# A six-block decoder on one core: order of the keys inside a head, and how the values of the first attention are loaded

## The chip, the cores and the metric

The kernel runs on one core of one Trainium2 chip. The metric is the device time of one launch in microseconds (us). Three runs of the kernel before gave 284.87, 285.77 and 710.45 us; the median is 285.77 us, and the third run is one outlier. A profiled execution was taken apart from them.

## The reference

Eight sequences of 128 tokens with 128 features pass through six blocks; after each block the input is added and the sum is layer-normalised. Only the first block is touched here:

```
xq = einsum('bsh,oh->bso', x, wq)          # 8 x 128 x 1024, the same for xk, xv
xq = xq.reshape(bsz, 16, seqlen, 64)       # no transpose: a plain reshape
scores = softmax(einsum('bhid,bhjd->bhij', xq, xk) * 64 ** -0.5)
out = einsum('bhij,bhjd->bhid', scores, xv).reshape(bsz, seqlen, 1024)
x = layernorm(x + einsum('bso,ho->bsh', out, wo))
```

The reshape has no transpose. So head n of a sequence is made of the eight tokens 8n to 8n+7: its row j is the 64 features of column block c (of 16) of token 8n+t, with j = 16t + c. Softmax and the weighted sum run over all 128 rows of keys, so the rows of the keys may be stored in any order as long as the values have the same one.

The other five blocks are a cross-attention, a gated expert, a causal attention of 16 heads of 8 features, a rotary cross-attention with decay, and a quantised feed-forward.

## The kernel before, in words

Each engine has a program of its own, written out by hand; semaphores join them. Time is counted in ticks t. The first attention works on pairs of sequences p = 0 to 3 (NPAIR), with 32 heads per pair, 4 heads per tick (one quad Q), so 8 ticks per pair (QP) and 32 ticks in all. Projections of pair p+1 stand in the ticks of pair p, by the table PJ: i = 0 to 3 are the four projections of the keys, 4 to 7 those of the queries, 8 to 11 those of the values. Ticks 0 and 1 of a pair hold the four of the keys, 2 and 3 those of the queries, 3, 4 and 7 those of the values. Pair 0 is projected before tick 0.

For a projection of keys or queries TensorE (`project`, L618 to L620) writes 512 columns of one PSUM bank. ScalarE (`empty_projection`, L1056) copies it as f16 into the upper halves, VectorE (`lower_parts`, L1305) subtracts that from the PSUM value and stores the rest as f16: what the f16 could not hold. Both do this in two instructions per projection of 64 partitions x 512 elements, one for each half of the column blocks (a = 0, 1). A pair has 8 such instructions for the keys on each engine, and 8 for the queries; four pairs have 64 on each. Two PSUM banks are used in turn: project(i) waits until VectorE has done projection i-2.

The keys lie in KA (upper parts in partitions 0 to 63, lower parts in 64 to 127), the queries in QS; both are parts of the tile `arena`. The view `by_column` says where an element goes. A column block is c = 8a + g. Inside a head of 128 elements, before, the order is (a, g, t): t runs fastest, so eight tokens are 16 bytes in a row. Every read of KA or QS by TensorE is a whole head, so it does not depend on the order inside it.

SyncE (SP) issues all DMAs, one after the other. For each pair: copies of KA into KB with the halves swapped (L374, L376); two stores of the values from VN to `v_piece` in HBM (L383); then for each half h of the heads the loads into V (L390), eight per half, one for each t, each of 16 column blocks x 16 heads x 64 elements into the partitions t, 8+t, 16+t and so on. The partitions of V are the key rows in the order of KA. TensorE's `weigh` (L665) multiplies the exponentials (PT) with V and waits for a half's loads through `v_load`, at 128 per pair (8 x 16).

Behind the last pair's V loads SP goes on to the second attention: constants `later` into the stacks of its first group (L400, waits for `sk_done` 24), stores of its keys and queries (L404, L407, wait for `kp_hi`, `qp_hi` and so on), and, when the stores have landed, loads into the stacks (L410, L414). TensorE's first scores of that attention (`scores1`, L782) wait for all of them at tick 32. Group means the sequences 0 to 2; mid(g, i) are the steps of blocks 2 and 3 of group g, which stand between the others by the table PLACES.

Of the kernel before, what the change touches and what calls it, by code (L numbers as in the profile page):

```python
# [14 lines left out]
P = 128  # L15
NB = 8
NTOK = NB * P
H = 16
DH0 = 64
G = 8  # L20
# [33 lines left out]
def decoder(nc, x_tok, x_T, ctx_T, wq0, wk0, wv0, wo0, xwq0, xbq0, xwk0, xbk0, xwv0, xbv0,  # L54
# [6 lines left out]
    with ExitStack() as ctx:  # L61
# [123 lines left out]

            return buf[:, n * P:(n + 1) * P]

        def by_column(buf, i):

            v = buf.rearrange("p (n a g t) -> p a g n t", a=2, g=G, t=8)  # L190
            return v[:, :, 2 * (i % 4):2 * (i % 4) + 2, :, :]

        def bank(i):
# [5 lines left out]
        def s(name):  # L199

            if name not in named:
                named[name] = sem(name)
            return named[name]
# [114 lines left out]

        def v_there(p, q):

            return s(f"v_load{p % 2}{q // 4}"), 128 * (p // 2 + 1)

        def projected_at(p, i):

# [14 lines left out]
        def _(sp):  # L339
# [31 lines left out]
            for p in range(NPAIR):  # L371
                b = p % 2
                sp.wait_ge(s("qk_hi"), 8 * p + 4)
                sp.dma_start(KB[b][64:P, :], KA[b][0:64, :]).then_inc(qk_in[b], 16)  # L374
                sp.wait_ge(*((pj_free[1], 6 * (p - 1) + 2) if p else (s("qk_lo"), 4)))
                sp.dma_start(KB[b][0:64, :], KA[b][64:P, :]).then_inc(qk_in[b], 16)  # L376
                if p == 1:
                    load_first()
                if p == 2:
                    load_rest()  # L380
                for h in range(2):
                    sp.wait_ge(*((pj_free[1], 6 * (p - 1) + 5 + h) if p else (s("vn_in"), 2 * h + 2)))
                    sp.dma_start(v_piece[2 * p + h].rearrange("n (t c) d -> (n t) (c d)", t=8), v_half(h))\  # L383
                        .then_inc(s(f"v_out{h}"), 16)
                for h in range(2):
                    sp.wait_ge(s(f"v_out{h}"), 16 * (p + 1))
                    if p >= 2:
                        sp.wait_ge(s("pv_done"), QP * (p - 1))
                    for t in range(8):
                        sp.dma_start(V[t::8, b, h * H:(h + 1) * H, 0:DH0],  # L390
                                     v_piece[2 * p + h].rearrange("n (t c) d -> t c n d", t=8)[t])\
                            .then_inc(s(f"v_load{b}{h}"), 16)

# [636 lines left out]
        def _(act):  # L1032
# [14 lines left out]
            def empty_projection(p, i):  # L1047
                at = projected_at(p, i)
                src = bank(at).rearrange("p (g n t) -> p g n t", g=2, t=8)
                act.wait_ge(s("proj_done"), NPROJ * p + i + 1)  # L1050
                if i < 8:
                    if p >= 2:
                        act.wait_ge(s("sk_done"), QP * (p - 1))
                    dst = by_column((KA, QS)[i // 4][p % 2][0:64, :], i)
                    for a in range(2):
                        m = fn(dst[:, a], src[a * 64:(a + 1) * 64], ACT.Copy)  # L1056
                    m.then_inc(s("qk_hi"), 1)
                else:
                    h = (i - 8) // 2
                    if p and i % 2 == 0:  # L1060
                        act.wait_ge(s(f"v_out{h}"), 16 * p)
                    fn(v_half(h)[:, (i % 2) * 512:(i % 2) * 512 + 512], bank(at), ACT.Copy)\  # L1062
                        .then_inc(s("vn_in") if p == 0 else pj_free[i % 2], 1)
# [208 lines left out]
        def _(dve):  # L1272
# [27 lines left out]
            def lower_parts(p, i):  # L1300
                src = bank(projected_at(p, i)).rearrange("p (g n t) -> p g n t", g=2, t=8)
                dve.wait_ge(s("qk_hi"), 8 * p + i + 1)
                upper, lower = (by_column((KA, QS)[i // 4][p % 2][x, :], i) for x in (slice(0, 64), slice(64, P)))
                for a in range(2):
                    m = tt(lower[:, a], src[a * 64:(a + 1) * 64], upper[:, a], ALU.subtract)  # L1305
                m.then_inc(s("qk_lo") if p == 0 else pj_free[i % 2], 1)
# [428 lines left out]
```

## Time and profile before

| | us |
|---|---|
| three runs | 284.87, 285.77, 710.45 |
| median | 285.77 |
| profiled execution, whole | 287.07 |
| its span, first to last instruction | 285.3 |
| TensorE busy with matmuls | 232.6 (82%) |
| VectorE busy | 200.9 (70%) |
| ScalarE busy | 153.7 (54%) |
| GpSimd busy | 61.2 (21%) |

The profiled execution was 287.07 us, of which 285.3 us is the span. A busy share is a mean over stages with different limits. So the stages are read one by one: in which an engine is never idle, and where the busiest engine stands waiting, and for whom. In this profile PE is TensorE, DVE VectorE, ACT ScalarE, POOL GpSimd, and SPq the queue on which SyncE issues DMAs.

### The profile page before, as it was taken

To read this page: it belongs to the slowest core of one execution; us is meant where nothing else is said; L and a number is where in the kernel's file an instruction comes from. 1 tells how busy PE (TensorE), PEld (TensorE's weight loads), DVE (VectorE), ACT (ScalarE), POOL (GpSimd) and SP (SyncE) were. 2 spreads that over 40 slices of the span, in tenths; PEclk is the share of its full clock that TensorE was granted. 3 is DMA by queue.
4 is the path that set the end of the run, shared out by engine and by line. 5 is a ranking of instruction groups with operands and counts; after the bars stand their busy time and mean duration, and the time that the engine had idled before them with its cause. 6 is when DMAs were issued, how large, how long until landed. Compare 5 with 4: busy or idle time off the path is not lost.

```text
span 285.3 us, 6881 instructions
## 1 busy us (share of the span) xinstructions
PE 232.6 (82%) x2662; PEld 186.8 (65%) x2662; DVE 200.9 (70%) x535; ACT 153.7 (54%) x288; POOL 61.2 (21%) x108
## 2 busy tenths in 40 slices
PE   1869889989899999997994979979998887765442
PEld 1737767879698896986873847757765755453221
DVE  2695996479855989756443547567777878778896
ACT  4983765385737866463544125645643266551372
POOL 4698000000003001030212031443520101011133
PEclk9959999999999999999998689999999999987555
DMA  6265496147763471044979917920040000000002
GB/s 190 105 147 186 100 241 254 62 105 165 208 186 104 102 167 76 3 124 92 247 194 155 231 28 153 187 68 2 15 107 0 3 3 0 2 0 0 0 10 64
DMA packets 28495, 29.15 MB, mean 102 GB/s; under 512 B 19248, under 2 KB 24496, under 8 KB 27184
## 3 DMA queue, kind: packets, MB, share of 16 engines
q1 hardware_dynamic: 28464, 28.72, 39.6%
q8 instruction: 21, 0.34, 0.5%
q14 instruction: 10, 0.08, 0.1%
HBM read 18.49 MB, written 6.03 MB: 86 GB/s over the span
## 4 chain that ended last, share of the span: by engine, by line
PE 47%; DVE 25%; DMA 8%; ACT 6%; issue 6%; SPq 6%; POOL 1%; POOLq 0%; DVEq 0%
DVE arena L1305 7%; DMA k_piece<-VN 4%; PE PS L665 4%; SPq L390 4%; ACT arena L1056 3%; PE PS L799 3%; PE PS L589 3%; PE PS L692 3%; PE PS L782 2%; PE PS L633 2%; DMA arena<-q_piece 2%; PE PS L779 2%; PE PS L780 2%; PE PS L610 2%; DVE arena L1480 2%
## 5 line engine op out<-in xcount | busy, mean ns | idle before, releaser
L1305 DVE TENSOR_TENSOR arena<-PS,arena 64x512 f16<-64x512 f32 x64 | 44.1, 690 | 9.8 <-ACT arena L1056 8.5
L1056 ACT ACTIVATE arena<-PS 64x512 f16<-64x512 f32 x64 | 37.8, 591 | 11.7 <-PE PS L620 10.6
L494 POOL TENSOR_SCALAR shift<-mv 128x3 f32<-128x3 f32 (+2 forms) x12 | 2.9, 241 | 161.4 <-DVE mv L1357 161.4
L1145 ACT ACTIVATE PT<-PS 128x512 f32<-128x512 f32 x32 | 19.0, 594 | 19.9 <-PE PS L783 19.5
L1442 DVE TENSOR_REDUCE rowmax<-PS 128x4 f32<-128x512 f32 x32 | 21.7, 682 | 10.8 <-PE PS L783 10.7
L618 PE MATMUL PS<-xh,w0l 128*128 128x256 f32 x64 | 20.8, 324 | 7.8 <-DVE w0l L1296 5.7
L665 PE MATMUL PS<-V,PT 128*64 128x68 f32 x512 | 22.7, 232 | 3.0 <-issue 1.8
L1310 DVE TENSOR_REDUCE rowmax<-PS 128x4 f32<-128x512 f32 x32 | 21.7, 683 | 2.9 <-PE PS L634 2.5
L1069 ACT ACTIVATE PT<-PS 128x512 f32<-128x512 f32 x32 | 19.0, 595 | 8.7 <-PE PS L649 7.6
L647 PE MATMUL PS<-arena 128*128 128x128 f16 x128 | 23.3, 221 | 0.1
L649 PE MATMUL PS<-MR,En 128*128 128x128 f16 x128 | 23.1, 219 | 0.0
L648 PE MATMUL PS<-arena 128*128 128x128 f16 x128 | 23.1, 219 | 0.0
L665 PEld LDWEIGHTS PS<-V,PT 128*64 128x64 f32 x512 | 18.2, 139 | 7.1 <-issue 3.1
L618 PEld LDWEIGHTS PS<-xh,w0l 128*128 128x128 f32 x64 | 12.8, 200 | 9.1 <-DVE w0l L1296 5.7
L619 PE MATMUL PS<-xl,w0h 128*128 128x256 f32 x64 | 18.6, 290 | 0.0
L620 PE MATMUL PS<-xh,w0h 128*128 128x256 f32 x64 | 18.5, 290 | 0.0
L633 PE MATMUL PS<-arena 128*128 128x128 f16 x128 | 17.9, 221 | 0.5 <-DVE rowmax L1310 0.5
L780 PE MATMUL PS<-MR,En 128*128 128x128 f16 x128 | 18.0, 221 | 0.0
L634 PE MATMUL PS<-arena 128*128 128x128 f16 x128 | 17.6, 219 | 0.0
L1089 ACT ACTIVATE xt<-res,shift,rstd 128x128 f32<-128x128 f32 x32 | 13.5, 484 | 6.3 <-POOL shift L497 6.2
L692 PE MATMUL PS<-wo,OT 128*128 128x128 f32 x128 | 16.0, 278 | 0.5 <-ACT OT L1079 0.4
L1062 ACT ACTIVATE VN<-PS 128x512 f32<-128x512 f32 x16 | 9.4, 597 | 12.7 <-PE PS L612 12.4
(229 smaller groups left out, 631.7 us busy)
## 6 DMA issues: line engine op xcount, KB each, us to landing
arena<-later SPq DMA_DIRECT2D x4, 1152.0 KB, 10.7
arena<-arena SPq DMA_DIRECT2D x8, 512.0 KB, 5.4
v_piece<-VN SPq DMA_DIRECT2D x8, 512.0 KB, 3.0
V<-v_piece SPq DMA_DIRECT2D x64, 64.0 KB, 2.5
V<-later SPq DMA_DIRECT2D x2, 768.0 KB, 10.9
arena<-k_piece SPq DMA_DIRECT2D x4, 192.0 KB, 4.8
arena<-q_piece SPq DMA_DIRECT2D x4, 192.0 KB, 6.0
q_piece<-VN SPq DMA_DIRECT2D x6, 96.0 KB, 5.7
```

Of the source, the lines that this page charges most:

```text
L618: mm(dst, w0l[:, w, g], xh[:, x], start=True, stop=False)
L633: mm(dst, head(QS[p % 2], n), head(KB[p % 2], n), start=True, stop=False)
L647: mm(dst, head(KB[p % 2], n), head(QS[p % 2], n), start=True, stop=False)
L648: mm(dst, head(KA[p % 2], n), head(QS[p % 2], n), start=False, stop=False)
L649: m = mm(dst, En[:, n % H, :], MR[:, b % 2, :], start=False, stop=True)
L665: m = mm(bank(4)[h * 64:h * 64 + 64, first:first + VN_COLS], PT[:, Q % SLOTS_PT, n * P + a * 64:n * P + a * 64 + 64], V[:, p % 2, 4 * q + ...
L692: m = mm(bank(5)[:, 0:P], OT[:, b % 2, g, :], wo[:, g, :], start=(g == 0), stop=(g == G - 1))
L780: mm(part_, En[:, n, :], MR[:, b % 2, :], start=False, stop=False)
L1056: m = fn(dst[:, a], src[a * 64:(a + 1) * 64], ACT.Copy)
L1305: m = tt(lower[:, a], src[a * 64:(a + 1) * 64], upper[:, a], ALU.subtract)
L1310: V_.reduce_max(rowmax[:, 4 * Q:4 * Q + 4], tok(bank(quad_bank(Q))), AX_X)\
L1442: V_.reduce_max(rowmax[:, b * H + 4 * q:b * H + 4 * q + 4], tok(bank(w % 3)), AX_X)\
```

## The change

The keys get another order inside a head: (t, a, g), which is t x 16 + c, the order of the reference. The queries keep theirs. With that, the 128 rows of a head in `v_piece` are in the order of the partitions of V, and a half's values come by one DMA in place of eight. The semaphore then counts 16 per pair in place of 128.

```
-        def by_column(buf, i):
-            v = buf.rearrange("p (n a g t) -> p a g n t", a=2, g=G, t=8)
+        def by_column(buf, i, keys=False):
+            order = "n t a g" if keys else "n a g t"
+            v = buf.rearrange(f"p ({order}) -> p a g n t", a=2, g=G, t=8)
             return v[:, :, 2 * (i % 4):2 * (i % 4) + 2, :, :]
...
-            return s(f"v_load{p % 2}{q // 4}"), 128 * (p // 2 + 1)
+            return s(f"v_load{p % 2}{q // 4}"), 16 * (p // 2 + 1)
...
-                    for t in range(8):
-                        sp.dma_start(V[t::8, b, h * H:(h + 1) * H, 0:DH0],
-                                     v_piece[2 * p + h].rearrange("n (t c) d -> t c n d", t=8)[t])\
-                            .then_inc(s(f"v_load{b}{h}"), 16)
+                    sp.dma_start(V[:, b, h * H:(h + 1) * H, 0:DH0], v_piece[2 * p + h].rearrange("n j d -> j n d"))\
+                        .then_inc(s(f"v_load{b}{h}"), 16)
...
-                    dst = by_column((KA, QS)[i // 4][p % 2][0:64, :], i)
+                    dst = by_column((KA, QS)[i // 4][p % 2][0:64, :], i, i < 4)
...
-                upper, lower = (by_column((KA, QS)[i // 4][p % 2][x, :], i) for x in (slice(0, 64), slice(64, P)))
+                upper, lower = (by_column((KA, QS)[i // 4][p % 2][x, :], i, i < 4) for x in (slice(0, 64), slice(64, P)))
```

In the view of the keys one instruction now steps 16 f16 elements (32 bytes) from each element to the next, where eight neighbours stood together before. The number of elements and of bytes is the same everywhere, and a packet of the V loads stays one row of 64 f32, 256 bytes.

On SP's queue, in the program of the last pair and the start of the second attention's first group, this stood before (V is loaded from v_piece, `later` holds constants of the stacks):

```order
L383 DMA v_piece<-VN 128x1024 x2
L390 DMA V<-v_piece 16x16x64 x16
L400 DMA arena<-later 96x6144 x2
L404 DMA k_piece<-VN 128x384 x2
L407 DMA q_piece<-VN 128x384 x3
```

and this stands there now:

```order
L390 DMA V<-v_piece 128x16x64 x2
L399 DMA arena<-later 96x6144 x2
L403 DMA k_piece<-VN 128x384 x2
L406 DMA q_piece<-VN 128x384 x3
L409 DMA arena<-k_piece 16x6144 x2
```

Fourteen issues are gone ahead of the constants; nothing has changed its place. (Line numbers behind the V loads are one lower in the new file.)

On DVE's queue, at the start (pair 0's lower parts, the first maxima, then pair 1's first lower parts), this stood before:

```order
L1305 TENSOR_TENSOR arena<-PS,arena 64x2x32x8 x16
L1310 TENSOR_REDUCE rowmax<-PS 128x4 x5
L1316 TENSOR_SCALAR MR<-PS 16x128
L1317 SCALAR_TENSOR_TENSOR MR<-PS,MR 16x128
L1305 TENSOR_TENSOR arena<-PS,arena 64x2x32x8 x4
L1310 TENSOR_REDUCE rowmax<-PS 128x4
```

and this stands there now:

```order
L1304 TENSOR_TENSOR arena<-PS,arena 64x2x256 x8
L1304 TENSOR_TENSOR arena<-PS,arena 64x2x32x8 x8
L1309 TENSOR_REDUCE rowmax<-PS 128x4 x5
L1315 TENSOR_SCALAR MR<-PS 16x128
L1316 SCALAR_TENSOR_TENSOR MR<-PS,MR 16x128
L1304 TENSOR_TENSOR arena<-PS,arena 64x2x256 x4
```

The instructions are as many and in the same order; those of the keys have another form: 2 x 256 elements at an even step in place of 2 x 32 runs of 8. ScalarE's queue changes in the same way.

## Rows read from the trace of the kernel before

**Rows 1.** The chain that ended last, shares of the span by line (the page).

```profile
DVE arena L1305 7%; DMA k_piece<-VN 4%; PE PS L665 4%; SPq L390 4%; ACT arena L1056 3%; PE PS L799 3%; PE PS L589 3%; PE PS L692 3%; PE PS L782 2%; PE PS L633 2%; DMA arena<-q_piece 2%; PE PS L779 2%; PE PS L780 2%; PE PS L610 2%; DVE arena L1480 2%
```

**Rows 2.** Busy time of DVE in five stretches: from:to, length, busy, PE clock, DMA.

```profile
9.30:21.20 11.90, 11.04 (x16) 0.76 0.39 90
28.20:43.40 15.20, 14.19 (x24) 1.00 0.70 174
43.40:58.80 15.40, 7.48 (x20) 1.00 0.42 152
58.80:75.20 16.40, 14.94 (x27) 1.00 0.67 161
92.80:110.30 17.50, 16.13 (x31) 1.00 0.47 110
```

**Rows 3.** Timeline of SP, 123 to 136 us: start, length, line, what.

```profile
123.54 11.20 SPq L390 DMA_DIRECT2D V<-v_piece  x16
134.79 1.06 SPq L400 DMA_DIRECT2D arena<-later  x2
```

**Rows 4.** The chain in order of time, 136 to 164 us.

```profile
136.36 11.61 DMA k_piece<-VN
150.63 5.91 DMA arena<-q_piece
158.47 0.85 PE PS L709 x3
```

**Rows 5.** Timeline of PE and ACT: in brackets the idle time before, and its releaser.

```profile
131.71 0.69 PE L665 MATMUL PS<-V,PT 128*64 128x68 f32 x16 [1.78 <-issue]
155.36 1.26 ACT L1089 ACTIVATE xt<-res,shift,rstd 128x128 f32<-128x128 f32 x3 [1.47 <-POOL shift L497]
156.68 0.59 PE L782 MATMUL PS<-arena 128*128 128x128 f16 x4 [3.42 <-DMA arena<-q_piece]
167.43 1.10 PE L709 MATMUL PS<-ident,xt 128*128 128x128 f32 x3 [1.99 <-ACT xt L1089]
```

**Rows 6.** DMA issues of the page: what, how many, size, median time to landing.

```profile
V<-v_piece SPq DMA_DIRECT2D x64, 64.0 KB, 2.5
arena<-later SPq DMA_DIRECT2D x4, 1152.0 KB, 10.7
arena<-arena SPq DMA_DIRECT2D x8, 512.0 KB, 5.4
```

**Rows 7.** Groups of the two instructions: busy, mean ns of one | idle before, releaser.

```profile
L1305 DVE TENSOR_TENSOR arena<-PS,arena 64x512 f16<-64x512 f32 x64 | 44.1, 690 | 9.8 <-ACT arena L1056 8.5
L1056 ACT ACTIVATE arena<-PS 64x512 f16<-64x512 f32 x64 | 37.8, 591 | 11.7 <-PE PS L620 10.6
L1296 DVE TENSOR_TENSOR w0l<-w,w0h 128x512 fp32r<-128x512 f32 x2 | 1.4, 692 | 1.2 <-ACT w0h L1039 1.2
```

**Rows 8.** Groups with long and short steps, kept apart by form (columns as Rows 7).

```profile
L459 POOL MEMSET V<- 128x2048 f32 x1 | 1.8, 1804 | 0.0
L452 POOL MEMSET ident<- 128x128 f32 x1 | 0.2, 204 | 0.3 <-POOLq L1728 0.3
L460 POOL MEMSET V<- 128x64 f32 x1 | 0.2, 207 | 0.1
L486 POOL MEMSET arena<- 128x32 f32 x1 | 0.2, 168 | 0.0
L1457 DVE RECIPROCAL rec<-PS 128x16 f32<-128x16 f32 x8 | 2.0, 255 | 3.3 <-PE PS L844 3.1
L1333 DVE RECIPROCAL rec<-PS 128x4 f32<-128x4 f32 x32 | 5.7, 178 | 12.5 <-PE PS L665 12.1
L1518 DVE RECIPROCAL sm<-sm 128x4 f32<-128x4 f32 x1 | 0.2, 179 | 0.0
L1488 DVE RECIPROCAL hs<-hs 128x1 f32<-128x1 f32 x8 | 1.3, 164 | 0.3
```

**Rows 9.** Timeline of DVE and PE, 9 to 18 us.

```profile
14.07 7.09 DVE L1305 TENSOR_TENSOR arena<-PS,arena 64x512 f16<-64x512 f32 x10 [0.46 <-ACT arena L1056]
17.03 0.77 PE L610 MATMUL PS<-w0l,xh 128*128 128x512 f32 x1 [4.03 <-DVE arena L1305]
```

## The prediction, made before the changed kernel was run

> **What bounds the kernel now.** I read the chain that ended last first. It names VectorE's lower parts as its largest line, and close behind it three things that belong to SP and its DMAs: the store to k_piece, the issues of the V loads, and the load of the stacks [rows 1]. So the change touches both ends of this list: it takes issues from SP and it gives VectorE's largest line another access pattern.
>
> Then the busy time of VectorE by stretches [rows 2]. Pair 0's lower parts (9.3 to 21.2 us) and the three stretches in which the keys and queries of pairs 1 to 3 are projected leave VectorE 0.9, 1.0, 1.5 and 1.4 us free of 11.9, 15.2, 16.4 and 17.5. In them VectorE is the bound. In between (43.4 to 58.8 us) it is busy for 7.5 of 15.4 us, and something else sets the time. At 17.03 us TensorE stands idle for 4.03 us until a lower part is done [rows 9]: pair 0 has no other work in hand.
>
> Last, SP's queue and who waits for it. Pair 3's sixteen V loads are issued from 123.54 to 134.74 us, 0.70 us each, and only then the constants of the second attention's first group [rows 3]. Two waits of TensorE follow. At 131.71 us `weigh` begins after 1.78 us of idle time for which the profile shows no engine [rows 5]. The eighth load is issued at about 123.54 + 7 x 0.70 = 128.4 us and lands some 2.5 us later [rows 6], near 131: I read this as a wait for V. At 156.68 us the first scores of the second attention start 3.42 us late, named as a wait for the stack load [rows 5]; behind it stand 5.91 us of that load and 11.61 us in which the store to k_piece lay behind the constants [rows 4].
>
> **What the change takes away.** 64 issues become 8; for a pair, 14 issues x 0.70 us = 9.8 us of SP's queue. For pair 3 the constants can be issued near 124.8 us in place of 134.79; their semaphore (`sk_done` 24) is reached about when the last values are projected, and the keys' parts that L404 waits for come soon after. The one transfer of a half has 512 KB; a copy of that size lands in 5.4 us at the median [rows 6], so half 0 is there at about 123.54 + 5.4 = 128.9 us, and the 1.78 us go. What is late next there is TensorE's own work. For the stacks the constants' transfer of 10.7 us stays, and about 5 us of V transfers stand before it in the same queue: end near 124 + 5 + 10.7 = 140 us, the k_piece store right behind it, near 141, then 2 us of issues, and 5.9 us of the load as now: 149 to 150 us in place of 156.5. TensorE would want it at 156.68 - 3.42 - 1.78 = 151.5 us. So that wait goes too, with a margin under 2 us.
>
> But not all of 3.42 us is won. Two steps later TensorE turns group 1's x at 158.47 us [rows 4], and this x is ready at 155.36 + 1.26 = 156.62 us [rows 5]. What is late next is this chain of ScalarE and VectorE; from 158.47 only 1.85 us can go. TensorE's own work up to the next turn doesn't count, since at 167.43 it waits 1.99 us for the same chain [rows 5]. Gain: 1.78 + 1.85 = 3.6 us. The other pairs' V loads and the earlier KB copies I set at nothing: the chain of waits names none of them. If the margin of 2 us is gone, the second term shrinks to nothing and the gain is 1.8 us.
>
> **What it adds.** No instruction, but 32 of L1305's 64 and 32 of L1056's 64 now step 32 bytes per element. At present a lower part takes 690 ns, as much as a plain subtraction of 512 contiguous f32, 692 ns [rows 7]: runs of eight cost nothing. The trace has no 512-element instruction with a long step, so I bound it by the few short ones [rows 8].
> - From below: 4 elements at a step of 384 bytes take 178 ns, 4 contiguous ones 179 ns. Nothing added; a gain has no reason, since the count of elements is the same.
> - VectorE's reciprocal of 16 elements at a step of 32 bytes takes 255 ns. Contiguous ones rise from 164 to 179 ns from 1 to 4 elements, 5 ns each, which makes 239 ns for 16. Left over: 16 ns, 1.0 ns per element. By the slope between the stepped ones, (255 - 178) / 12 = 6.4, it is 1.4 ns, the upper end.
> - GpSimd's memset of 64 elements at a long step takes 207 ns, of 128 contiguous ones 204 ns. Contiguous ones cost (1804 - 204) / 1920 = 0.83 ns each, so 64 would take 151 ns: 0.87 ns more per element. By the slope of the stepped ones alone, (207 - 168) / 32 = 1.22, it is 0.39 ns more.
> I take 1.0 ns for VectorE, the row with the very step of 32 bytes and on the very engine, and 0.87 ns for ScalarE, for which there is no row: 690 becomes 1200 ns, 591 becomes 1040 ns. The ends are 0 and 1.4 ns (1410 ns).
>
> The Trainium skill, page "Advanced Engine Details and Errata", section "SBUF Cachelines", speaks against this change: SBUF is read and written in lines of 16 bytes, and an access is at full rate only if the next one falls into the same line; at least two hits per line are needed. Eight f16 fill one line in the old order, and in the new one no two neighbours share one. The page gives no figure for this; by it the added cost would be there, and the small stepped rows above agree in sign. No row at 512 elements shows it.
>
> Now along the path. Pair 0: 8 x 0.51 = 4.1 us more on VectorE, which starts 2 x 0.45 = 0.9 us later since ScalarE's first two copies are longer, less the 0.46 us that it idles today [rows 9]: 4.5 us, and TensorE waits for exactly this. Pairs 1 to 3: 4.1 + 0.9 = 5.0 us each, less what is free in the stretch, 1.0, 1.5 and 1.4 us, all of which I let it swallow: 4.0 + 3.5 + 3.6 = 11.1 us. ScalarE gains 8 x 0.45 = 3.6 us of work per pair, which lies beside VectorE's. The stretches in between can't give this back, because they are bound by other engines. Sum: 4.5 + 11.1 = 15.6 us.
>
> **Sum.** +15.6 - 3.6 = +12.0 us. Against the profiled execution: 287.07 + 12.0 = 299.1 us; it stood 1.3 us above the median of the runs, so in runs 285.77 + 12.0 = 297.8 us. Its own range: the cost swings from 12 us (VectorE's free time and the order of ticks hide more) to 20 us (nothing is swallowed), the gain from 1.8 to 5 us: 293 to 302.
>
> **Rivals.**
> - A smaller step cost, 0.4 ns per element as by the slope of the memsets: 0.2 us per instruction, 1.6 us for pair 0 and, since the free time swallows a larger share, 1.2 us for each other pair: 5.2 - 3.6 = +1.6, 287.4 us. For it: one of two readings of the GpSimd rows. Against it: VectorE's own row.
> - No step cost. Then the gain alone remains, 285.77 - 3.6 = 282.2 us, 1.3% faster. For it: the pair of 4-element rows, and that the kernel's f16 output today costs no more than f32. Against it: both longer rows.
> - Clearly faster: no step cost, and TensorE gets the full 3.42 us at the second attention because the chain of x moves up as well: 1.78 + 3.42 = 5.2, and half a microsecond from the V loads of each of pairs 1 and 2: 285.77 - 6.2 = 279.5 us. Against it: the stretch's later wait of 1.99 us.
> - That the transfer of one piece is no earlier (half 0 needs all 128 partitions before the first `weigh` of a pair) would cost the 1.78 us and, at pairs 0 to 2, nothing, since eight loads were all needed before too. It moves each case by under 2 us.
>
> **Chances.** The forecast 0.48, smaller cost 0.20, no cost 0.25, clearly faster 0.07. A measurement of this kernel tells about 2% from no change: under 280.1 us is faster, over 291.5 us slower. Slower: the forecast's 0.48 and 0.05 of the smaller cost with a larger share on the path, 0.53; faster 0.06; within 2% 0.41. The range must reach down to the case of no cost, and up almost to the forecast's own end: 281 to 301.
>
> **What would show it.** The group of L1304, kept apart by form: the key form near 1200 ns and the query form still 690; L1055 near 1040. Pair 0's lower parts should end near 25.7 us in place of 21.2. VectorE's free time in the three stretches should be near nothing. SP's V loads should be 8 issues, the constants of the first group should follow pair 3's V loads at once, and L782 should begin without a wait for the stack load. If the key form stays under 750 ns, the forecast is wrong and the time is near 282; if it is over 1200 but the time rises by less than 8 us, then VectorE was less of a bound in the three stretches than its busy share says.

## The result, and the profile after

| | before | after |
|---|---|---|
| median of the runs | 285.32 us (4 runs) | 354.77 us (4 runs) |
| ratio, 95% interval | | 1.2441 [1.2346, 1.2537] |
| profiled execution, its span | 287.07, 285.3 us | 354.82, 353.0 us |

The changed kernel is slower by 69.5 us, 24%. The forecast was +12.0 us. The four runs of the kernel before hold the one outlier of 710.45 us; without it their median is 284.87 us. Later runs of it gave 285.34 and 285.57 us, against which the experiments are measured.

First its page, at the head: the span, the busy time of each engine, the granted clock in forty slices.

```profile
span 353.0 us, 6825 instructions
PE 252.0 (71%) x2662; PEld 203.6 (58%) x2662; DVE 252.8 (72%) x535; ACT 209.6 (59%) x288; POOL 61.4 (17%) x108
PEclk9955875569965699968599999889999999998655
```

VectorE has 51.9 us more work than before, ScalarE 55.9 us more, for the same number of instructions. TensorE has 19.4 us more, and it too has no new instruction: the clock line says why. The digits of 5 and 6 stand in slices 3 and 4, 7 to 9, 12 to 14, 18 and 20 (8.8 us each), which is where the keys of pairs 0 to 3 and part of the queries are projected; those of the last three slices stood there before too.

The page's groups of the two instructions (columns as in [rows 7], which they answer to):

```profile
L1304 DVE TENSOR_TENSOR arena<-PS,arena 64x512 f16<-64x512 f32 x64 | 96.3, 1504 | 29.6 <-ACT arena L1055 28.6
L1055 ACT ACTIVATE arena<-PS 64x512 f16<-64x512 f32 x64 | 93.5, 1460 | 25.5 <-PE PS L619 24.6
```

A mean of 1504 ns over 64 is a mixture, since only half of them are keys. The instructions of one line in a short stretch take it apart. Of L1055 from 8.3 to 12.9 us (pair 0's first keys), of L1304 from 20 to 28 us (keys) and from 33 to 40 us (queries); the three numbers are the least, the median and the largest duration in ns:

```profile
L1055 ACT ACTIVATE arena<-PS x2: 2368/2400/2431, 8.4 to 10.8; 64x512 f16<-64x512 f32 x2
...
L1304 DVE TENSOR_TENSOR arena<-PS,arena x4: 2284/2312/2330, 17.9 to 24.9; 64x512 f16<-64x512 f32 x4
...
L1304 DVE TENSOR_TENSOR arena<-PS,arena x8: 684/690/695, 32.8 to 37.8; 64x512 f16<-64x512 f32 x8
```

The keys' form takes 2312 ns, the queries' form 690 as ever. So each key instruction costs 1.62 us more on VectorE and about 1.74 us more on ScalarE (2.33 - 0.59). The two copies from 8.4 us on run while VectorE has nothing to do yet, and they are no faster: the two engines do not slow each other down here, the instruction is slow by itself.

What this does to the order of work is seen in pair 2. The timeline of ACT, DVE and PE, 93 to 119 us:

```profile
93.14 9.31 ACT L1055 ACTIVATE arena<-PS 64x512 f16<-64x512 f32 x4
104.17 4.71 ACT L1055 ACTIVATE arena<-PS 64x512 f16<-64x512 f32 x2 [1.11 <-PE PS L619]
109.40 4.68 ACT L1055 ACTIVATE arena<-PS 64x512 f16<-64x512 f32 x2
...
97.83 9.35 DVE L1304 TENSOR_TENSOR arena<-PS,arena 64x512 f16<-64x512 f32 x4 [5.09 <-ACT arena L1055]
114.11 4.67 DVE L1304 TENSOR_TENSOR arena<-PS,arena 64x512 f16<-64x512 f32 x2 [0.55 <-ACT arena L1055]
...
102.48 0.58 PE L617 MATMUL PS<-xh,w0l 128*128 128x256 f32 x1 [6.81 <-DVE arena L1304]
103.94 0.33 PE L646 MATMUL PS<-arena 128*128 128x128 f16 x1
113.62 0.58 PE L617 MATMUL PS<-xh,w0l 128*128 128x256 f32 x1 [1.81 <-DVE arena L1304]
```

A bank goes round: TensorE projects into it (102.48), ScalarE empties it (104.17 to 108.88), VectorE empties it (108.91 to 113.56), and TensorE may write again (113.62): 11.1 us a round, and since there are two banks, one projection in 5.6 us. VectorE's own work in this time is hardly less. Its window from the first to the last lower part of pair 2's keys, and the line with which the same work ended in the kernel before:

```profile
97.80:118.80 21.00, 19.77 (x11) 0.59 0.14 30
62.99 2.82 DVE L1305 TENSOR_TENSOR arena<-PS,arena 64x512 f16<-64x512 f32 x4
```

Of 21.0 us it is busy for 19.8; its two waits for ScalarE, 0.46 and 0.55 us, are what the round costs on top of its work. The other part of the loss is that it can't begin before ScalarE's first two copies are done, 4.7 us after 93.14. From the first key copy to the first projection of values pair 2 now takes 127.88 - 93.14 = 34.7 us; before it took 73.71 - 57.64 = 16.1, so 18.7 us are lost in this pair. Two lines of before, from its timeline of PE, enclose the same six multiplications of a key projection:

```profile
60.32 0.39 PE L618 MATMUL PS<-xh,w0l 128*128 128x256 f32 x1
61.14 0.23 PE L647 MATMUL PS<-arena 128*128 128x128 f16 x1
```

Before they took 0.82 us, after 103.94 - 102.48 = 1.46. The window of PE over these keys in the kernel after (columns as [rows 2], with PE's busy time), and, from its timeline, the 16 multiplications of L691 in the queries behind them:

```profile
92.00:116.00 24.00, 13.59 (x119) 0.67 0.30 67
121.17 3.29 PE L691 MATMUL PS<-wo,OT 128*128 128x128 f32 x16
```

TensorE had stood idle for 6.81 us before 102.48, and after it the multiplications have the length of the lower of the two levels (0.58 us for one, 1.2 GHz, against 0.36 to 0.39 at 2.4 GHz). Over this stretch 0.67 was granted; in the stretches of keys and queries before it was 1.00 [rows 2]. The waiting is the larger part of the loss, and the clock comes on top: 0.6 us in the key projection that lies on the path, and 1.3 us in L691, whose 16 multiplications took 2.00 us at the same place before (68.28 us).

Pair 0 has nothing to put between. Its timeline of DVE and PE, which answers to [rows 9]:

```profile
13.20 13.97 DVE L1304 TENSOR_TENSOR arena<-PS,arena 64x512 f16<-64x512 f32 x6 [5.83 <-ACT arena L1055]
28.16 10.36 DVE L1304 TENSOR_TENSOR arena<-PS,arena 64x512 f16<-64x512 f32 x10 [0.98 <-ACT arena L1055]
...
34.38 0.77 PE L609 MATMUL PS<-w0l,xh 128*128 128x512 f32 x1 [20.26 <-DVE arena L1304]
```

TensorE goes on at 34.38 in place of 17.03 us: 17.35 us late. In the chain that ended last ScalarE now leads: on the page its shares by line begin so (answers to [rows 1]).

```profile
ACT arena L1055 15%; DVE arena L1304 11%; PE PS L691 4%; PE PS L664 4%; PE PS L588 3%; PE PS L798 2%; PE PS L632 2%; PE PS L617 2%; PE PS L781 2%; PE PS L683 2%; PE PS L633 2%; PE PS L778 2%; PE PS L779 2%; PE PS L646 1%; DMA w<-wq 1%
```

What was to be gained did come. SP's queue behind pair 3 (answers to [rows 3]), and the page's line on the V loads (to [rows 6]):

```profile
195.14 3.56 SPq L390 DMA_DIRECT2D V<-v_piece  x2
198.75 2.68 SPq L399 DMA_DIRECT2D arena<-later  x2
```

```profile
V<-v_piece SPq DMA_DIRECT2D x8, 512.0 KB, 4.9
```

Two issues where sixteen stood, the constants right behind them, and in PE's timeline no wait is left at pair 3's first `weigh` nor at L781, where [rows 5] had 1.78 and 3.42 us.

### The profile page after: what moved, and what is told of

Same layout as the page of the kernel before. It is cut to its first block, busy times and chain, and to the rows that moved or that the text cites. A ratio compares the mean times of both kernels' runs of the same rounds, so it can differ in the third digit from the quotient of the medians.

```text
span 353.0 us, 6825 instructions
## 1 busy us (share of the span) xinstructions
PE 252.0 (71%) x2662; PEld 203.6 (58%) x2662; DVE 252.8 (72%) x535; ACT 209.6 (59%) x288; POOL 61.4 (17%) x108
## 4 chain that ended last, share of the span: by engine, by line
PE 47%; DVE 24%; ACT 18%; issue 7%; DMA 1%; POOL 1%; SPq 0%; POOLq 0%; DVEq 0%; ACTq 0%
ACT arena L1055 15%; DVE arena L1304 11%; PE PS L691 4%; PE PS L664 4%; PE PS L588 3%; PE PS L798 2%; PE PS L632 2%; PE PS L617 2%; PE PS L781 2%; PE PS L683 2%; PE PS L633 2%; PE PS L778 2%; PE PS L779 2%; PE PS L646 1%; DMA w<-wq 1%
## 5 line engine op out<-in xcount | busy, mean ns | idle before, releaser
L1304 DVE TENSOR_TENSOR arena<-PS,arena 64x512 f16<-64x512 f32 x64 | 96.3, 1504 | 29.6 <-ACT arena L1055 28.6
L1055 ACT ACTIVATE arena<-PS 64x512 f16<-64x512 f32 x64 | 93.5, 1460 | 25.5 <-PE PS L619 24.6
L617 PE MATMUL PS<-xh,w0l 128*128 128x256 f32 x64 | 25.0, 390 | 44.9 <-DVE arena L1304 39.2
L617 PEld LDWEIGHTS PS<-xh,w0l 128*128 128x128 f32 x64 | 16.3, 255 | 48.4 <-DVE arena L1304 42.6
L646 PE MATMUL PS<-arena 128*128 128x128 f16 x128 | 26.6, 239 | 0.1
L647 PE MATMUL PS<-arena 128*128 128x128 f16 x128 | 26.4, 237 | 0.0
L648 PE MATMUL PS<-MR,En 128*128 128x128 f16 x128 | 26.3, 237 | 0.0
L609 PE MATMUL PS<-w0l,xh 128*128 128x512 f32 x16 | 8.6, 537 | 22.2 <-DVE arena L1304 22.2
L618 PE MATMUL PS<-xl,w0h 128*128 128x256 f32 x64 | 22.3, 349 | 0.0
L664 PEld LDWEIGHTS PS<-V,PT 128*64 128x64 f32 x512 | 19.4, 147 | 5.0 <-issue 2.8
L619 PE MATMUL PS<-xh,w0h 128*128 128x256 f32 x64 | 22.3, 348 | 0.0
L632 PE MATMUL PS<-arena 128*128 128x128 f16 x128 | 19.7, 234 | 0.5 <-DVE rowmax L1309 0.5
L633 PE MATMUL PS<-arena 128*128 128x128 f16 x128 | 19.6, 234 | 0.0
L691 PE MATMUL PS<-wo,OT 128*128 128x128 f32 x128 | 17.8, 297 | 0.4 <-ACT OT L1078 0.4
L609 PEld LDWEIGHTS PS<-w0l,xh 128*128 128x128 f32 x16 | 3.3, 207 | 25.4 <-issue 21.9
```

Of the source, the lines that this page charges most:

```text
L617: mm(dst, w0l[:, w, g], xh[:, x], start=True, stop=False)
L618: mm(dst, w0h[:, w, g], xl[:, x], start=False, stop=False)
L619: m = mm(dst, w0h[:, w, g], xh[:, x], start=False, stop=True)
L632: mm(dst, head(QS[p % 2], n), head(KB[p % 2], n), start=True, stop=False)
L633: m = mm(dst, head(QS[p % 2], n), head(KA[p % 2], n), start=False, stop=True)
L646: mm(dst, head(KB[p % 2], n), head(QS[p % 2], n), start=True, stop=False)
```

## Experiments

Nine more kernels were run. Three of them (load alone, lower old, upper old) move part of the keys or values to other rows than the rest, as said with each; the two probes leave the whole computation out and only time single instructions.

**One load per half, keys in the old order.** The load of the changed kernel in the kernel before, and with it the count of its semaphore (16 in place of 128). The values then meet other keys than their own, with the same amount of work.

```
-                    for t in range(8):
-                        sp.dma_start(V[t::8, b, h * H:(h + 1) * H, 0:DH0],
-                                     v_piece[2 * p + h].rearrange("n (t c) d -> t c n d", t=8)[t])\
-                            .then_inc(s(f"v_load{b}{h}"), 16)
+                    sp.dma_start(V[:, b, h * H:(h + 1) * H, 0:DH0], v_piece[2 * p + h].rearrange("n j d -> j n d"))\
+                        .then_inc(s(f"v_load{b}{h}"), 16)
```

> The kernel before with the one load per half, and the keys in their old order, so the values meet the wrong keys (their order is left unmatched; no instruction is left out). If the stepped writes are the whole loss and SP's queue the whole gain: the time is 3.6 us below before (1.78 at pair 3's first weigh, 1.85 at the turn of group 1's x), a ratio of 0.987, and no wait for a stack load stands before the first scores of the second attention. Rival 1, one large transfer is no earlier than eight: ratio 1.00. Rival 2, the gain is larger since the chain of x moves too: 5 to 6 us, ratio 0.98. If part of the 69 us came from the load itself, this is slower than before.

Measured: 280.49 us against 285.57, ratio 0.9832 [0.9794, 0.9871]; 4.8 us (3.7 to 5.9) faster. Its timelines of SP and of PE, 122 to 164 us:

```profile
122.91 3.51 SPq L389 DMA_DIRECT2D V<-v_piece  x2
126.47 2.70 SPq L398 DMA_DIRECT2D arena<-later  x2
142.69 0.77 SPq L412 DMA_DIRECT2D arena<-q_piece  x2
...
153.35 0.71 PE L707 MATMUL PS<-ident,xt 128*128 128x128 f32 x2 [1.06 <-ACT xt L1087]
161.89 1.10 PE L707 MATMUL PS<-ident,xt 128*128 128x128 f32 x3 [1.21 <-ACT xt L1087]
```

Both waits are gone, and what is late next is x, as the prediction had it. The whole loss of the change is therefore in the order of the keys: 354.77 against 280.49 us, 74 us.

**The new order of keys alone.** The changed kernel with eight loads per half, each of 16 neighbouring partitions (and the count of 128 again).

```
-                    sp.dma_start(V[:, b, h * H:(h + 1) * H, 0:DH0], v_piece[2 * p + h].rearrange("n j d -> j n d"))\
-                        .then_inc(s(f"v_load{b}{h}"), 16)
+                    for t in range(8):
+                        sp.dma_start(V[16 * t:16 * t + 16, b, h * H:(h + 1) * H, 0:DH0],
+                                     v_piece[2 * p + h].rearrange("n (t c) d -> t c n d", t=8)[t])\
+                            .then_inc(s(f"v_load{b}{h}"), 16)
```

> The changed kernel with eight loads per half as before (partitions 16t to 16t+15), keys in the new order. If the new key order is the whole loss: key instructions near 2.3 us on ScalarE and VectorE, and 355 us plus what the single load gives, 2 to 4 us: 356 to 359 us. If the load had a part in the loss: clearly under 355 us.

Measured: 354.52 us, ratio 1.2432 [1.2365, 1.2499], below what was expected and level with the changed kernel. Its groups are those of the changed kernel (L1306, 1504 ns; L1057, 1459 ns). But both waits are there, in its timeline of PE:

```profile
202.55 0.69 PE L666 MATMUL PS<-V,PT 128*64 128x68 f32 x16 [0.78 <-issue]
226.46 0.57 PE L783 MATMUL PS<-arena 128*128 128x128 f16 x4 [2.42 <-DMA arena<-q_piece]
```

Yet these 3.2 us do not show in the total. The two intervals, some 2 and 3 us to each side, leave room for most of it, and part is won back: the first scores begin 3.7 us later than in the changed kernel (226.46 against 222.78 us), but the second turn of x behind them is only 1.6 us later (236.56 against 234.98), since TensorE waits for x there in both, 2.05 and 2.06 us. What stands is that the order of the keys makes the whole loss.

**Only ScalarE's half of the new order.** VectorE reads the upper parts in the new order and writes the lower parts in the old one, which puts them into other rows than their upper parts.

```
-                upper, lower = (by_column((KA, QS)[i // 4][p % 2][x, :], i, i < 4) for x in (slice(0, 64), slice(64, P)))
+                upper = by_column((KA, QS)[i // 4][p % 2][0:64, :], i, i < 4)
+                lower = by_column((KA, QS)[i // 4][p % 2][64:P, :], i)
```

> The changed kernel, but VectorE writes the lower parts of the keys in the old order; it still reads the upper parts at the step of 32 bytes, and ScalarE still writes them so (the lower parts of the keys are in the wrong places). Theory W, the price is on writes to SBUF alone: VectorE's key instructions fall from 2.3 us to about 0.7, ScalarE's stay at 2.3, time near 315 us. Theory R, stepped reads cost too: VectorE's key instructions stay above 1.2 us.

Measured: 339.62 us in one run, 25 us over the expectation. VectorE's lower parts from 13 to 24 us, and, from the timelines of ACT and DVE, the beginning and the end of pair 2's keys:

```profile
L1305 DVE TENSOR_TENSOR arena<-PS,arena x6: 1056/1060/1105, 13.2 to 23.5; 64x512 f16<-64x512 f32 x6
...
87.63 9.38 ACT L1055 ACTIVATE arena<-PS 64x512 f16<-64x512 f32 x4
107.47 2.14 DVE L1305 TENSOR_TENSOR arena<-PS,arena 64x512 f16<-64x512 f32 x2 [3.01 <-ACT arena L1055]
```

With VectorE's write back in the old order its key instruction falls from 2312 to 1060 ns, 0.37 us over the old 690. So the stepped read of f16 costs 0.37 us when it stands alone. It is no part of the 1.62 that adds up with the write: the first probe below has 2285 ns with both and 2284 with the write alone. And although VectorE is so much lighter, the kernel is only 15 us faster than the changed one. Pair 2's keys take from 87.63 to 109.61 us, 22.0 us, against 8.2 in the kernel before (57.64 to 65.81): 13.8 more, which is 8 x 1.74 of ScalarE. ScalarE alone holds it up.

**Only VectorE's half.** Upper parts written and read in the old order, only the lower parts written in the new one (again in other rows than their upper parts).

```
-                    dst = by_column((KA, QS)[i // 4][p % 2][0:64, :], i, i < 4)
+                    dst = by_column((KA, QS)[i // 4][p % 2][0:64, :], i)
...
-                upper, lower = (by_column((KA, QS)[i // 4][p % 2][x, :], i, i < 4) for x in (slice(0, 64), slice(64, P)))
+                upper = by_column((KA, QS)[i // 4][p % 2][0:64, :], i)
+                lower = by_column((KA, QS)[i // 4][p % 2][64:P, :], i, i < 4)
```

> The changed kernel, but ScalarE writes the upper parts of the keys in the old order and VectorE reads them so; only VectorE's lower parts are written stepped (the upper parts of the keys are in the wrong places). Key instructions 591 ns on ScalarE, 2285 on VectorE. If VectorE is the bound in the four projection stretches: 8 x 1.6 = 12.8 us for each, less its free time (0.9, 1.0, 1.5, 1.4 us), less the gain of the load of 5 us: 285.6 + 46 - 5 = 327 us. If ScalarE's and VectorE's longer instructions add up one behind the other (two PSUM banks in turn), then the losses of this kernel and of the one with old lower parts are each well under 69 us and together more than it.

Measured: 335.57 us in one run, 8.6 us over the expectation. The page's groups, and again the beginning and the end of pair 2's keys:

```profile
L1305 DVE TENSOR_TENSOR arena<-PS,arena 64x512 f16<-64x512 f32 x64 | 96.5, 1509 | 11.0 <-ACT arena L1055 9.8
L1055 ACT ACTIVATE arena<-PS 64x512 f16<-64x512 f32 x64 | 37.9, 592 | 48.1 <-PE PS L619 47.3
...
83.27 2.42 ACT L1055 ACTIVATE arena<-PS 64x512 f16<-64x512 f32 x4
95.17 9.33 DVE L1305 TENSOR_TENSOR arena<-PS,arena 64x512 f16<-64x512 f32 x4
```

Against the kernel with the load alone (280.5 us) VectorE's slow writes cost 55 us, ScalarE's (with VectorE's slower read) 59 us, both together 74. They overlap by 40 us: 74 is 19 more than VectorE alone.

The keys of pair 2 say where the 19 come from. Here they take from 83.27 to 104.50 us, 21.2 us, 13.1 more than before: 8 x 1.64 of VectorE, which does not wait once it has begun (no bracket in its line). In the changed kernel they take from 93.14 to 118.78 us, 25.6 us, so 4.4 more: 3.5 for the two copies that VectorE must see done before it begins, and 1.0 for its two waits. Of ScalarE's 13.9 us of new work per pair the other 9 or so are hidden beside VectorE's. Four pairs at 4.4 us make some 18 of the 19. (The two kernels with half of the new order have one run each, so the 55 and 59 are rougher than the other differences; the lengths within a pair are read from one trace each.)

**Single instructions, first probe.** 512 elements of f32 from PSUM into SBUF, by ScalarE (copy) and by VectorE (minus an SBUF operand), at every step in question; each one waits for the one before, each shape twice. `hf` is an f16 tile, `full` an f32 tile, `up` an f16 tile that VectorE reads; `every(x, s)` takes every s-th element, and `link` makes the next instruction wait for this one.

```
+            link(fn(every(hf, 1), src, ACT.Copy))     # the same for 2, 4, 8, 12, 16, 17, 32, and for full
+            link(fn(keys(hf), src4, ACT.Copy))        # also queries, and pairs (g innermost)
+            link(tt(every(hf, 1), src, every(up, 16), ALU.subtract))
```

> Not the decoder: 512-element instructions on 64 partitions, one after the other, first on ScalarE (PSUM to SBUF), then on VectorE (subtraction with a second source in SBUF), at several steps, in f16 and f32; the rest of the computation is left out. Theory W (an element written into another 16-byte line than the one before costs about 4.5 ns, on both engines, whatever its width or step): f16 steps 1 to 4 take 590 ns on ScalarE and 690 on VectorE, step 8 and more 2300; f32 from step 4 on 2300; reads at step 16 add little. Theory N (narrow: only writes of less than 4 bytes suffer): f32 at a step of 32 bytes stays at 600 to 700 ns, f16 is slow from step 2 on. Theory B (banks: steps that are powers of two suffer): steps 12 and 17 stay under 1000 ns. Theory R: read 16, write 1 takes over 1200 ns. The pairs form (runs of two f16 in a line) should cost half of the keys form under W, 1.2 to 1.4 us. A read of PSUM at a step of 128 bytes is unknown: 590/690 ns if it is free.

Measured, from the trace's groups by line (mean ns of one; the second instruction of each shape agreed within 2 ns):

| written | f16 on ScalarE | f16 on VectorE | f32 on ScalarE |
|---|---|---|---|
| step 1 | 591 | 682 | 591 |
| step 2 | 731 | 718 | 612 |
| step 4 | 1294 | 1283 | 1059 |
| step 8 | 2424 | 2412 | 1077 |
| step 12 | 2403 | 2389 | |
| step 16 | 2297 | 2284 | 1017 |
| step 17 | 2324 | 2310 | |
| step 32 | 2382 | 2370 | |
| form of the keys | 2297 | 2285 | |
| pairs, g innermost | 622 | 684 | |

Four of the rows behind it: ScalarE, f16 at steps 4 and 8, f32 at step 8, and VectorE with a read at step 16 and a write at step 1.

```profile
L76 ACT ACTIVATE hf<-PS 64x512 f16<-64x512 f32 x1 | 2.4, 2424 | 0.0
L92 ACT ACTIVATE full<-PS 64x512 f32<-64x512 f32 x1 | 1.1, 1077 | 0.0
L126 DVE TENSOR_TENSOR hf<-PS,up 64x512 f16<-64x512 f32 x1 | 1.1, 1056 | 0.0
L74 ACT ACTIVATE hf<-PS 64x512 f16<-64x512 f32 x1 | 1.3, 1294 | 0.0
```

Lone f16 (no neighbour written with them) at steps 2, 4 and 8 touch 128, 256 and 512 pieces of 16 bytes, and 168 ns + 4.4 ns per piece, fitted to these three, gives 731, 1294 and 2421 against 731, 1294 and 2424: the time follows these pieces, not the elements. Beyond step 8, where every element has a piece of its own, the step hardly matters, and an odd step (17) is no better than a power of two (16), which speaks against a conflict of memory banks (theory B). An f32 at a step of 32 bytes takes 1077 ns on ScalarE, 0.95 ns per element over the 591, and 1068 ns on VectorE, 0.75 ns over the 682 (that is the contiguous f16; contiguous f32 was 692 ns in [rows 7]). So not the step alone is dear, but the narrow write: an f32, a whole 4-byte word, costs about a quarter of the extra. A PSUM read with a step costs nothing (591 and 683 ns). No theory of the four was right alone.

**g innermost.** With the same order of keys in memory, and so the same single load, two neighbouring column blocks g are written by one instruction. If g runs fastest in the instruction, two f16 are one word.

```
+            if i < 4:
+                v = buf.rearrange("p (n t a g) -> p a n t g", a=2, g=G, t=8)
+                return v[:, :, :, :, 2 * (i % 4):2 * (i % 4) + 2]
...
+        def as_written(bank_, i):
+            return bank_.rearrange("p (g n t) -> p n t g" if i < 4 else "p (g n t) -> p g n t", g=2, t=8)
...
-                src = bank(at).rearrange("p (g n t) -> p g n t", g=2, t=8)
+                src = as_written(bank(at), i)
```

> The changed kernel, with the same order of the keys (t, a, g), but each instruction writes it with g innermost: runs of two f16, one whole 4-byte word, at a step of 32 bytes; PSUM is read at a step of 1 KB instead. Theory P (what costs is a lone f16 in a 16-byte line, about 4.4 ns per line; whole 4-byte words cost at most 2 ns per line): key instructions near 620 ns on ScalarE and 685 on VectorE, as in the list of steps, and the whole gain of the single load: 280 to 281.5 us, ratio 0.983. Rival Q (the cheap form holds only for an engine alone; both engines writing to one tile, or PSUM read stepped while TensorE fills another bank, costs more): key instructions over 900 ns and more than 290 us.

Measured: 281.56 us against 285.34, ratio 0.986 [0.9816, 0.9904]. The eight key instructions of pair 3 on each engine, from 91 us on (least, median, largest ns):

```profile
L1310 DVE TENSOR_TENSOR arena<-PS,arena x8: 685/695/703, 92.7 to 99.0; 64x512 f16<-64x512 f32 x8
L1061 ACT ACTIVATE arena<-PS x8: 630/642/686, 91.4 to 97.7; 64x512 f16<-64x512 f32 x8
```

Same bytes at the same places, another order of writing them: VectorE is back at 695 ns and ScalarE at 642 (the means over keys and queries together are 690 and 619), 73 us come back, and this kernel keeps the gain of the load. It is faster than both kernels, than the one before by 4.0 us (2.7 to 5.3, by the ratio).

**The same with eight loads** (the diff of the load is that of the keys alone).

> The new order of the keys written in pairs, with eight loads per half: ratio 1.00 to 1.004 if the order is free in that form (30 ns more per ScalarE instruction) and all of the gain is the single load's; ratio near 0.983 if the gain came from the order.

Measured: 283.18 us, ratio 0.9914 [0.9884, 0.9944], faster than expected. Its timelines of SP and PE:

```profile
124.38 9.35 SPq L397 DMA_DIRECT2D V<-v_piece  x16
...
131.83 0.69 PE L672 MATMUL PS<-V,PT 128*64 128x68 f32 x16 [1.08 <-issue]
156.03 0.38 PE L789 MATMUL PS<-arena 128*128 128x128 f16 x4 [2.72 <-DMA arena<-q_piece]
```

Sixteen issues take 9.35 us, 0.58 each, where those that took every eighth partition took 0.70 [rows 3]. By the ratios 2.5 us of the gain come with the order of the rows, eight loads being still there, and 1.5 us more with one load in place of eight; the two intervals overlap by a little, so the second share is the less certain. The two waits are 0.7 us shorter each than before (1.08 against 1.78, 2.72 against 3.42); where the rest of the 2.5 us comes from is not shown.

**Constants ahead of the last V loads.** The kernel before, with the constants of the second attention's first group issued between the two halves of pair 3's V loads.

```
+                    if p == NPAIR - 1 and h == 1:
+                        constants(0)
                     sp.wait_ge(s(f"v_out{h}"), 16 * (p + 1))
```

> The kernel before with one thing changed: SP issues the constants of the second attention's first group between the two halves of pair 3's V loads, eight issues earlier, and no load of V is merged. If the stack's wait is half of the gain or more: the wait of 3.42 us before the first scores goes, the 1.78 us before pair 3's first weigh stay, ratio 0.988 to 0.993. Rival: the second half's V loads now lie behind 2.3 MB of constants and weigh waits for them: ratio 1.00 or more.

Measured: 285.15 us against 285.34, ratio 0.9994 [0.996, 1.0028]: no difference, as the rival had it. Its timeline of PE:

```profile
131.33 0.69 PE L672 MATMUL PS<-V,PT 128*64 128x68 f32 x16 [1.81 <-issue]
145.38 0.91 PE L672 MATMUL PS<-V,PT 128*64 128x68 f32 x11 [2.49 <-issue]
```

The stack wait is gone, and in its place stands a wait of 2.49 us before `weigh` takes up the half of V that now lies behind the constants (read so from its place; the profile names no releaser). The last load of this half is issued at 138.8 us, and `weigh` begins at 145.38, 6.6 us later, while the median load of this size landed after 2.5 us in the kernel before [rows 6]. So it seems to wait for the transfer, beside the 2.3 MB of constants, and not for SP's issue. This other order of the issues gained nothing; fewer issues did.

**Single instructions, second probe.** Runs of f16 of several lengths, on a word's border or moved by one element, and 128 partitions in place of 64, 256 elements in place of 512.

```
+            link(fn(runs(hf, 2, 16, 0), cut(2), ACT.Copy))   # pairs on whole words, every 32 bytes
+            link(fn(runs(hf, 2, 16, 1), cut(2), ACT.Copy))   # the same, moved by one element
+            link(fn(every(hf, 16, 256), PS[0:64, 0, 0:256], ACT.Copy))
```

> Not the decoder: single instructions as in the first list, the rest of the computation is left out. Theory P as fitted to the first list: a 16-byte line that gets a lone f16 (half of a 4-byte word) costs 4.4 ns, a line that gets whole words only costs at most 2 ns, and an element never less than its own time; about 160 ns are fixed. Then for ScalarE: pairs on whole words at 32 or 16 bytes 590 to 680 ns; the same pairs moved by one element (two half words, one line) 160 + 256 x 4.4 = 1290; runs of 4 on whole words 590 to 620, moved by one element 160 + 128 x 4.4 = 720; lone elements on 128 partitions 2300 as on 64; 256 lone elements 1290; runs of 8 at 32 bytes 590. VectorE: the same, with 690 for 590. Rival L (the price is per line or run, whole words or not, and falls with the length of the run): the moved pairs cost as much as the aligned ones. If lone elements on 128 partitions cost twice, the limit is shared between partitions.

Measured on ScalarE, in ns: pairs on whole words 622, the same pairs moved by one element 1231, runs of four 590, runs of four moved 700, lone ones on 128 partitions 2303, 256 lone ones 1230. On VectorE: 683, 1260, not tried, 686, 2291, 1218. Two of the rows by line (moved pairs on ScalarE and on VectorE):

```profile
L80 ACT ACTIVATE hf<-PS 64x512 f16<-64x512 f32 x1 | 1.2, 1231 | 0.0
L114 DVE TENSOR_TENSOR hf<-PS,up 64x512 f16<-64x512 f32 x1 | 1.3, 1260 | 0.0
```

The pairs say it most plainly: same length, same step, same number of 16-byte pieces, and one element's shift doubles the time. A pair on a word's border costs nothing beyond 622 ns; 256 pairs that lie across two words cost as much as 256 lone elements (1230). It is the half-written word that is dear, once for each 16-byte piece with one in it.

## Why the prediction was wrong

**The cost per instruction.** This is the step that failed: "I take 1.0 ns for VectorE, the row with the very step of 32 bytes and on the very engine", and with it 690 to 1200 ns and 591 to 1040 ns. Measured: 2312 and 2330 ns, 3.2 and 3.4 ns per element, over the upper end of 1.4. The sign and the place were right, the size was three to four times too small. The row it was taken from was a reciprocal of f32 [rows 8]. The first probe gives for f32 at this very step (1077 - 591) / 512 = 0.95 ns per element on ScalarE and (1068 - 682) / 512 = 0.75 ns on VectorE, against the 0.87 and 1.0 that were taken for them. So the estimate was sound for f32 and could not hold for f16: the row had the engine and the step, but not the width of the element written, and that is what decides. The upper end of 1.4 ns was no bound for the same reason: every stepped row of the trace that timed a step wrote f32.

The Trainium skill, page "Advanced Engine Details and Errata", section "SBUF Cachelines", which the prediction weighed, had the direction right. But its rule of two hits per line did not hold for f16: at a step of 4 elements two lie in each 16 bytes, and ScalarE took 1294 ns in place of 591; f32 at a step of 2 elements, also two to a line, took 612.

**The path.** With the measured sizes in the prediction's own formula pair 0 comes to 8 x 1.62 + 2 x 1.74 - 0.46 = 16.0 us, and pairs 1 to 3 to 16.4 less 1.0, 1.5 and 1.4: together 61.4 us, and with a gain of 4 to 5 us a time near 342. Measured 354.8. The remaining 13 us come from smaller steps that failed.

The first is the free time: "less what is free in the stretch, 1.0, 1.5 and 1.4 us, all of which I let it swallow". Nothing was swallowed, for that free time did not lie among the keys. In the kernel before VectorE runs through pair 2's keys without a wait (58.87 to 65.81 us), and what is free in the stretch stands behind them, in the queries. With the 0.46 us of pair 0 that is 4.4 us.

The second is that ScalarE's work lies wholly "beside VectorE's". It mostly does (see the two kernels with one half slow), but once VectorE's instructions are as long as ScalarE's the round through two banks makes it wait, about 1 us per pair.
- In pair 0 ScalarE is the chain: 8 x 1.74 + 2 x 1.62 = 17.2 us, measured 17.35.
- From the first key copy to the last key difference the kernel before takes 8.0, 8.2 and 8.2 us in pairs 1 to 3, the kernel after 25.6 in each: 17.5 more. By VectorE's queue that is 3.5 of later start, 13.0 of its own work and 1.0 of waits. By the chain of pair 2 (two copies, two differences, TensorE's projection 2, its two copies, the two of projection 3, two differences) it is 6 x 1.74 + 4 x 1.62 = 16.9 us and 0.6 of TensorE's lower clock. Both sums meet the measured time, so the two paths are equally long here.
- The rest of pair 2's 18.7 us, 1.2, is lost in its queries: L691 took 3.29 us in place of 2.00, at the lower clock.
- All four pairs: 69.5 + 4.8 = 74.3 us of loss, of which pair 0 has 17.4 and pairs 1 to 3 on average 19.0. The keys themselves have 69.9 of it.

The forecast that VectorE's free time in these stretches would be near nothing was wrong. The kernel after has more of it: the windows of DVE from the first lower part of the keys to the end of the queries of pairs 1 to 3 (answers to [rows 2]):

```profile
48.60:79.00 30.40, 27.32 (x24) 0.55 0.32 96
97.80:127.00 29.20, 25.80 (x23) 0.65 0.29 71
149.80:182.00 32.20, 29.86 (x31) 0.73 0.16 34
```

3.1, 3.4 and 2.3 us are free, and before the first lower part VectorE has stood idle for 5 us besides. Within the keys it is busy for nine tenths and more and still sets the pace, with ScalarE just beside it.

**The gain.** Forecast 3.6 us; measured 4.8 (3.7 to 5.9) with the load alone and 4.0 (2.7 to 5.3) with g innermost. The mechanism was right in both places: SP's 14 issues less, the constants at 126.5 us in the load-alone kernel (forecast near 124.8), the last loads of the stacks issued at 142.69 us, 7 to 8 us sooner than before (150.17), both of TensorE's waits gone, x late next. The term of the second wait was somewhat too small: I held the time at which x is ready fixed at 156.62 us, but with the load alone it is turned at 153.35 and the later turn comes at 161.89 in place of 167.43, so the chain of x moved up as well. Counted from pair 3's first `weigh` in each trace (129.21 and 131.71 us) the turns come 2.6 and 3.0 us sooner, which with the 1.78 us makes the 4.8. The rival "clearly faster" named this point; its 6.2 us were 1.4 to 2.2 us too much. The rival that one transfer is no earlier did not come true: it landed after 4.9 us at the median, and TensorE did not wait for it. In the changed kernel itself the gain could not be seen in the total (the keys alone, 354.52 us).

**The rest of the checks.** The queries' form kept its 690 ns, the V loads were 8 issues, the constants followed at once, and L781 began without a wait. Pair 0's lower parts were to end at 25.7 us and ended at 28.16 + 10.36 = 38.5. One slip in the sums: with a cost of 20 and a gain of 1.8 us the forecast's own range ends at 304, not 302; it changes nothing here.

## What to carry to other kernels

Before a layout is changed to save DMAs, let the innermost run of every f16 write be a whole, aligned 4-byte word, by the order of the loops in the instruction if not by the layout: the same bytes in the same places took 2312 or 695 ns here on VectorE, 73 us in all. Take the cost of a stepped access only from a row that agrees in engine, in direction (read or write) and in the width of the element. Where several engines pass a few buffers round, add up one round, divide by the number of buffers and compare with the busiest engine's own work: the longer of the two sets the pace, here 11.1 us against some 10.6. Add the filling, since the second engine starts later by what the first has got slower, and subtract free time only where it lies among the instructions that get longer. Slowing the second engine too did not add its 59 us to the 55 of the first, but 19.

## What the runs showed of the hardware that was not expected

- A write of f16 that fills only half of a 4-byte word costs 4.2 to 4.4 ns for each 16 bytes in which that happens, on ScalarE ((2303 - 1230) / 256 = 4.2; (2424 - 1294) / 256 = 4.4) as on VectorE ((2291 - 1218) / 256 = 4.2; (2412 - 1283) / 256 = 4.4), alike on 64 and on 128 partitions (2297 and 2303 ns).
- Whole words at a step of 32 bytes cost less than 1 ns each more than contiguous ones when they are f32 (1077 against 591 ns for 512), and pairs of f16 on a word's border next to nothing (622 against 591 ns for 256 pairs).
- Reads of f16 at a step of 32 bytes cost VectorE 0.37 us per 512 elements (1056 against 682 ns) when the write is contiguous, and nothing on top of a slow write (2285 against 2284). Stepped reads of PSUM cost neither engine anything (591 and 683 ns).
- SP needs less time to issue a DMA into 16 neighbouring partitions (0.58 us) than one into every eighth (0.70 us), for the same bytes.
- After TensorE had stood idle for 6.81 us in pair 2, the next key projection took 1.46 us in place of 0.82; over the stretch of those keys the granted clock was 0.67, where it had been 1.00.
